# First attention: keys and queries as 64x64 products in four quarters of the array, two shared banks, another order of work

## The reference, cut to what matters

```python
q = einsum('oi,bil->bol', Wq, layernorm(x)) + bq      # k, v likewise from ctx
scores = einsum('hbdk,hbek->hbde', qh, kh) / 8        # 8 heads of 64 columns, 64 x 64 scores
x = x + Wo @ (softmax(scores) @ v) + bo
logits = layernorm(x) @ W_gate + b_gate               # top 2 of 8 experts, for the next phase
```

## Time and profile before

| | before |
|---|---|
| median of 3 runs | 995.98 us (995.69, 995.98, 999.72) |
| the profiled execution | 999.03 us, its span 997.2 us |
| PE busy over the span | 917.3 us (92%) |
| DVE, ACT, POOL busy | 440.8, 344.0, 290.4 us |
| scores of the first tile to the count product behind the last rank | 12.43 to 157.78 us |
| first work of PE for the experts | 169.97 us |
| clock granted to PE, mean | 0.949 |

### The profile page before, as it was taken

The page is one execution under the profiler, slowest core; times in us unless marked ns, Lnnn a source line. Parts: engine busy times, 40 slices in busy tenths (PEclk is TensorE's granted clock), DMA queues, the critical chain, the costliest instruction groups (busy, mean ns, idle before and its releaser), DMA issues. The chain is left out here.

```text
span 997.2 us, 17352 instructions
## 1 busy us (share of the span) xinstructions
PE 917.3 (92%) x6049; PEld 760.0 (76%) x6050; DVE 440.8 (44%) x888; ACT 344.0 (35%) x535; POOL 290.4 (29%) x416
## 2 busy tenths in 40 slices
PE   5999973999995889999999984999999999999997
PEld 4888863777774778888888863888788878878886
DVE  4888874333432546666666651212222222222112
ACT  3656631333331335565566542222111112111111
POOL 4678863000003554465564320211302000202000
PEclk9999985999997959999999985999999999999999
DMA  8566544444446532433433225111003000302001
GB/s 263 180 223 223 183 139 161 163 148 155 149 150 215 182 109 75 136 101 101 135 90 92 72 80 157 32 53 51 1 11 106 11 1 12 94 1 85 1 1 42
DMA packets 53431, 104.26 MB, mean 105 GB/s; under 512 B 7955, under 2 KB 8979, under 8 KB 53235
## 3 DMA queue, kind: packets, MB, share of 16 engines
q1 hardware_dynamic: 46594, 84.33, 26.6%
q0 software_dynamic: 5120, 16.78, 5.1%
q10 hardware_dynamic: 1648, 2.23, 0.6%
HBM read 65.83 MB, written 37.49 MB: 104 GB/s over the span
## 5 line engine op out<-in xcount | busy, mean ns | idle before, releaser
L1709 DVE SCALAR_TENSOR_TENSOR d_hid<-d_pup,d_b_up,d_silu 128x512 f32<-128x512 f32 (+1 forms) x44 | 33.0, 751 | 238.2 <-PE d_pup L1638 238.2
L1599 ACT ACTIVATE d_silu<-d_pgate,d_b_gate 128x512 f32<-128x512 f32 (+1 forms) x44 | 30.3, 689 | 154.7 <-PE d_pgate L1638 154.7
L985 POOL DMA_INDIRECT c_y_in<-expert_results,y_at x32 | 32.0, 999 | 152.9 <-POOLq L98 144.9
L1570 POOL TENSOR_TENSOR d_x_res<-d_x_res,d_b_down 128x512 f32<-128x512 f32 x16 | 21.2, 1350 | 188.2 <-DMA d_x_res<-x_after_attention 188.2
L1636 PE MATMUL d_pgate<-d_nT_hi,gate_up_hi 128*128 128x512 f32 (+1 forms) x176 | 71.5, 406 | 1.4 <-DVE d_nT_lo L1698 1.4
L1606 ACT ACTIVATE d_hid_hi<-d_hid 128x512 fp32r<-128x512 f32 (+1 forms) x44 | 27.8, 632 | 125.8 <-DVE d_hid L1709 125.8
L1638 PE MATMUL d_pgate<-d_nT_hi,gate_up_lo 128*128 128x512 f32 (+1 forms) x176 | 70.3, 400 | 0.0
L1637 PE MATMUL d_pgate<-d_nT_lo,gate_up_hi 128*128 128x512 f32 (+1 forms) x176 | 70.0, 398 | 0.0
L1636 PE MATMUL d_pup<-d_nT_hi,gate_up_hi 128*128 128x512 f32 (+1 forms) x176 | 69.7, 396 | 0.0
L1668 PE MATMUL d_pdown<-d_down_hi,d_hid_hi 128*128 128x512 f32 (+1 forms) x176 | 69.5, 395 | 0.0
L1638 PE MATMUL d_pup<-d_nT_hi,gate_up_lo 128*128 128x512 f32 (+1 forms) x176 | 69.3, 394 | 0.0
(11 more groups left out here) (227 smaller groups left out, 2077.8 us busy)
## 6 DMA issues: line engine op xcount, KB each, us to landing
b_rows<-expert_rows SPq DMA_DIRECT2D x39, 256.0 KB, 2.7
expert_results<-b_result SPq DMA_DIRECT2D x39, 256.0 KB, 2.0
a_wstage<-L_ffn_W_e SPq DMA_DIRECT2D x16, 512.0 KB
c_stage<-gate_up SPq DMA_DIRECT2D x16, 344.0 KB, 3.4
a_x<-x SPq DMA_DIRECT2D x16, 256.0 KB
a_ctx_in<-ctx SPq DMA_DIRECT2D x16, 256.0 KB
x_after_attention<-a_x SPq DMA_DIRECT2D x16, 256.0 KB
c_x<-x_after_attention SPq DMA_DIRECT2D x16, 256.0 KB, 2.9
```

What stands on the lines that cost most here:

```text
L985: pool.indirect_dma_start(out=y_in[:, 2 * (t % 2) + k, :], out_offset=None, in_=shared["ys"], in_offset=bass.IndirectOffsetOnAxis(ap=share ...
L1709: dve.scalar_tensor_tensor(hid[0:w, s % 2, :], pup[s % 2][0:w, :], b_up[0:w, i:i + 1], silu[0:w, s % 2, :], ALU.add, ALU.mult).then_inc(hi ...
```

## The change

- Keys and queries are no longer four products with a 128x128 weight each. Each is sixteen products of 64 rows, 64 columns and 64 moving columns: batch b (the rows of the array) and head parity r (its columns) pick one of the four quarters, in the order (0,0), (1,1), (0,1), (1,0).
- Both go to one tensor of two banks, `pkq`, batch b in bank b. So queries of a tile wait until its keys have been copied out, and keys wait for the copy of the queries before.
- The transposed normed result goes to `pt`, the bank of the transposed probabilities, in place of `pk`.
- Another order of the calls on PE, DVE and ACT. On PE: scores, keys, rank, values, transpose of the normed result, projection, queries, transpose of probabilities, logits, attention. In pvy the values of tile m+1 now come ahead of the projection of tile m-1, which waits until they have been copied out.

```diff
-        pk, pq, pvy, ps, pt, pr = (pb(n) for n in ("pk", "pq", "pvy", "ps", "pt", "pr"))
-        po = stack.enter_context(nc.psum_tensor("a_po", [P, 2, 512], F32))
+        pvy, ps, pt, pr = (pb(n) for n in ("pvy", "ps", "pt", "pr"))
+        pkq, po = stack.enter_context(nc.psum_tensor("a_pkq", [P, 2, 512], F32)), stack.enter_context(nc.psum_tensor("a_po", [P, 2, 512], F32))
...
# ACT, an iteration
-                if tile(m):
-                    high_part(m)
-                    exponent(m)
-                    keep_probT(m)
                 if tile(m + 1):
                     keep_v(m + 1)
+                if tile(m):
+                    exponent(m)
                 if tile(m - 2):
                     keep_xT(m - 2)
+                if tile(m):
+                    keep_probT(m)
+                    high_part(m)
...
# PE
+            def in_quarters(rows, w):
+                for j in range(4):
+                    for b, r in ((0, 0), (1, 1), (0, 1), (1, 0)):
+                        k, head = slice(64 * b, 64 * b + 64), 2 * j + r
+                        mm = pe.matmul(pkq[64 * r:64 * r + 64, b, 64 * j:64 * j + 64], rows[k, 64 * head:64 * head + 64],
+                                       w[k, k], start=True, stop=True)
+                return mm
...
# make_k
-                want(pe, k_kept, t)
-                want(pe, xt_kept, t - 3)
-                for j in range(4):
-                    mm = pe.matmul(pk[:, P * j:P * j + P], ctx_in[:, t % 3, P * j:P * j + P], wk[:, :], start=True, stop=True)
+                want(pe, q_kept, t)
+                mm = in_quarters(ctx_in[:, t % 3, :], wk)
# make_v
-                want(pe, x1_ready, t - 1)
+                want(pe, x1_ready, t - 2)
# make_q
-                want(pe, q_kept, t)
...
+                pe.wait_ge(k_kept, t + 1)
+                mm = in_quarters(xn[:, t % 2, :], wq)
# transpose_probs
+                want(pe, xt_kept, t - 1)
# project
-                if tile(t + 1):
-                    pe.wait_ge(v_kept, t + 2)
+                if tile(t + 2):
+                    pe.wait_ge(v_kept, t + 3)
# transpose_x
-                if tile(t + 3):
-                    pe.wait_ge(k_kept, t + 4)
+                if tile(t + 1):
+                    pe.wait_ge(pt_kept, t + 2)
...
# PE, an iteration, after
                     make_scores(m)
                     make_k(m + 1)
                     make_rank(group_ending(m - 3))
                     make_v(m + 1)
                     transpose_x(m - 2)
                     project(m - 1)
                     make_q(m + 1)
                     transpose_probs(m)
                     make_logits(m - 2)
                     make_attn(m)
# DVE, an iteration, after: sort, find, mark and add_marks of m-3 stay first, then
                     max_scores(m)
                     shift_scores(m)
                     keep_k(m + 1)
                     add_region(g), pick_ranks(g), sum_ranks(g), round_ranks(g)
                     add_residual(m - 1)
                     keep_q(m + 1)
                     sum_x1(m - 1), average_x1(m - 1)
                     sum_x(m + 3), average_x(m + 3)
                     invert_sums(m), keep_attn(m)
```

More of the change, by code:

```diff
@@ L365, in keep_xT @@
                 want(act, l_made, t)
-                act.activation(xT[:, :], pk[:, :], ACT.Copy).then_inc(xt_kept, 1)
+                act.activation(xT[:, :], pt[:, :], ACT.Copy).then_inc(xt_kept, 1)
             def high_part(t):
@@ L410, in make_q @@
                 pe.wait_ge(xn_ready, t + 1)
-                want(pe, q_kept, t)
-                for j in range(4):
-                    mm = pe.matmul(pq[:, P * j:P * j + P], xn[:, t % 2, P * j:P * j + P], wq[:, :], start=True, stop=True)
+                pe.wait_ge(k_kept, t + 1)
+                mm = in_quarters(xn[:, t % 2, :], wq)
                 mm.then_inc(q_made, 1)
@@ L461, in transpose_x @@
                 for j in range(4):
-                    mm = pe.transpose(pk[:, P * j:P * j + P], xn2[:, t % RING, P * j:P * j + P], ident[:, :])
+                    mm = pe.transpose(pt[:, P * j:P * j + P], xn2[:, t % RING, P * j:P * j + P], ident[:, :])
                 mm.then_inc(xt_made, 1)
@@ L491, in _ @@
                     make_scores(m)
-                if tile(m - 1):
-                    project(m - 1)
                 if tile(m + 1):
                     make_k(m + 1)
-                    make_q(m + 1)
-                if tile(m):
-                    transpose_probs(m)
+                if group_ending(m - 3) is not None:
+                    make_rank(group_ending(m - 3))
                 if tile(m + 1):
@@ L502, in _ @@
                     transpose_x(m - 2)
-                if group_ending(m - 3) is not None:
-                    make_rank(group_ending(m - 3))
+                if tile(m - 1):
+                    project(m - 1)
+                if tile(m + 1):
+                    make_q(m + 1)
+                if tile(m):
+                    transpose_probs(m)
+                if tile(m - 2):
+                    make_logits(m - 2)
                 if tile(m):
                     make_attn(m)
-                if tile(m - 2):
-                    make_logits(m - 2)
             pe.wait_ge(seen_ready, len(GROUPS))
@@ L526, in by_position, with made @@
             def by_position(ap):
-                return ap.rearrange("p (j o) -> p j o", o=64)
-            every_bk, every_bq = (b[:, :].rearrange("p (x o) -> p x o", x=1).to_broadcast([P, 8, 64]) for b in (bk, bq))
+                return ap.rearrange("p (j b o) -> p b j o", b=2, o=64)
+            def made():
+                return pkq[:, :, 0:256].rearrange("p b (j o) -> p b j o", o=64)
+            every_bk, every_bq = (b[:, :].rearrange("p (x y o) -> p x y o", x=1, y=1).to_broadcast([P, 2, 4, 64]) for b in (bk, bq))
             def keep_k(t):
@@ L535, in keep_k @@
                 want(dve, s_made, t)
-                dve.tensor_tensor(by_position(kT[:, :]), by_position(pk[:, :]), every_bk, ALU.add).then_inc(k_kept, 1)
+                dve.tensor_tensor(by_position(kT[:, :]), made(), every_bk, ALU.add).then_inc(k_kept, 1)
             def keep_q(t):
@@ L542, in keep_q @@
                 want(dve, s_made, t)
-                dve.tensor_tensor(by_position(qT[:, :]), by_position(pq[:, :]), every_bq, ALU.add).then_inc(q_kept, 1)
+                dve.tensor_tensor(by_position(qT[:, :]), made(), every_bq, ALU.add).then_inc(q_kept, 1)
             def max_scores(t):
@@ L640, in _ @@
                     shift_scores(m)
-                if tile(m - 1):
-                    add_residual(m - 1)
                 if tile(m + 1):
                     keep_k(m + 1)
[L645 to L649, removed]
                 if g is not None:
@@ L654, in _ @@
                     round_ranks(g)
+                if tile(m - 1):
+                    add_residual(m - 1)
+                if tile(m + 1):
+                    keep_q(m + 1)
+                if tile(m - 1):
+                    sum_x1(m - 1)
+                    average_x1(m - 1)
                 if tile(m + 3):
```

## The result

The kernel after takes 1010.96 us, the median of 4 runs (1005.99 to 1011.88); the kernel before, run on the same chip beside it, 997.69 (4 runs, 995.69 to 999.72). The ratio is 1.0123, with an interval from 1.008 to 1.0165: 1.2% slower, more than the spread of the runs. The forecast was 994.4 with a range to 1003. The profiled execution after took 1011.88 and has a span of 1010.1, so 12.9 more than before.

The account below looks back on a forecast made before the run. PE was taken to bound an iteration at 8.06, and afterwards the cycle PE, DVE, PE, ACT, PE at 8.37. Start +1.0, twelve iterations +1.8 and tail -4.4 gave -1.6: 994.4 from 995.98, range 987 to 1003.

Parts of the forecast that it names:

- the term of the twelve iterations: First attention, scores of tile 3 to those of tile 15: 12 x 8.37 = 100.4 against 98.63, +1.8.
- rival B: First attention: `low_part` on POOL holds DVE's `pick_ranks` in every tile; +13 in twelve iterations, 1007.5; chance 0.1.
- Two stalls: PE in each iteration: 0.38 ahead of the rank product for `add_marks`, 0.6 ahead of the projection for `keep_v`.
- The clean iteration: First attention, one tile's scores to the next: 8.37, where PE's own work is 7.23.
- Rival A: Keys and queries: column halves of the same rows don't run side by side, 0.030 a pass; +6.6, 1001.0; chance 0.2.
- Rival C: First attention: one of the two stalls is absent, POOL's 7.8 bounds; 12 x 0.57 less, 987.6; chance 0.22.
- Start: Start to the scores of tile 3: second iteration 7.3 against 6.34, +0.4 ahead of it, -0.4 in the third; +1.0.
- Tail: Behind tile 15's scores: no collision and attention at full clock, -2.7; clock staying up behind it, 1.7; together -4.4.
- Or if anything behind 170 us moves: Sign against the prediction: it is wrong if anything after 170 us moves.
- the sum: Whole kernel: +1.0 + 1.8 - 4.4 = -1.6, giving 994.4 on the median of 995.98; forecast's chance 0.42.

Follow-up runs that it names:

- with zeros: Kernel after, with POOL writing zeros into the experts' low part (two memsets) in place of the subtraction; one run, 1008.24, twelve iterations 102.77.
- with the wait: Kernel after, with POOL's `low_part` of tile m-1 waiting until `round_ranks` of tile m-3 is done; 1005.12, ratio 1.0041 to the kernel before.
- the ranks later on DVE: Kernel after, with `pick_ranks`, `sum_ranks` and `round_ranks` moved behind `average_x1` on DVE; 1008.65, ratio 1.0082 to the kernel before.
- the kernel before with the wait: Kernel before, with POOL's `low_part` of tile m-1 waiting until `add_marks` of tile m-3 is done; 995.27, ratio 0.9949 to the kernel before.
- the kernel with 128x128 products: Kernel after's order and waits, but keys and queries as four 128x128 products each; 1017.27, ratio 1.0169 to the kernel before.
- the clean tile above: A tile no hold lengthens, from kernel after with `pick_ranks`, `sum_ranks`, `round_ranks` behind `average_x1` on DVE; that kernel 1008.65, ratio 1.0082.
- the other order: Kernel after's quarters, PE, ACT and DVE reordered, ACT's `norm_x` earlier, `high_part` later, `low_part` waiting for ranks; fastest kernel measured, 996.58, ratio 0.9921 to before.

## Why the prediction was wrong

**The step that failed** is the term of the twelve iterations, "12 x 8.37 = 100.4 against 98.63: +1.8", which counts no held DVE instruction in any of them. It measured +17.5. The collision was looked for in the tail alone, and there for the marks alone: "POOL comes to that `low_part` about 3.9 after the scores and the marks are done at 2.0, so I expect no collision". For the tail this held: POOL came 4.95 after the scores of tile 15, and nothing was held there. For the steady tiles the collision was left to rival B, with a chance of 0.1 and a price of 13. B was the truth: 13.4 of the 17.5 in the twelve iterations go when `low_part` is made harmless in either of two ways (102.77 with zeros, 102.76 with the wait). That its price fits so well is in part luck: 3.2 of the 13.4 lie in the first iteration, where the marks are held and the clock falls, which B did not have. The places that B worked out were right to 0.2: `pick_ranks` at 3.94, forecast 4.1 to 4.35, and `low_part` at 4.38, forecast 4.4. With these a hold would still seem to be missed by 0.1 to 0.3, and I leaned on that. Two facts were not in the account.

First, DVE is held from a point ahead of the start that the profile shows for POOL's instruction. The cast of two neighbouring tiles, the first held, the second not:

```profile
72.58 3.08 DVE L640 CAST a_ati<-a_at_kept 128x2 int32<-128x2 f32 x1
73.25 2.39 POOL L303 TENSOR_TENSOR expert_w_lo<-a_wstage,expert_w_hi 128x1024 fp32r<-128x1024 f32 x1
...
82.27 0.96 POOL L310 DMA_INDIRECT expert_rows<-a_xn,a_ati  x1 [0.30 <-issue]
82.56 0.17 DVE L640 CAST a_ati<-a_at_kept 128x2 int32<-128x2 f32 x1
83.25 2.39 POOL L303 TENSOR_TENSOR expert_w_lo<-a_wstage,expert_w_hi 128x1024 fp32r<-128x1024 f32 x1
```

0.67 ahead it is held, 0.69 ahead it is not; the other tiles agree (held at 0.66 to 0.68, free at 0.69 to 0.84), each with a scatter right ahead of `low_part`. Is it then the scatter that holds DVE? Two runs answer: the ranks later on DVE, and the kernel before with the wait. In both, `mark_experts` begins 0.39 into a scatter that starts at 152.50 and at 132.83; in the second, `low_part` still waits for the marks:

```profile
152.89 2.98 DVE L607 TENSOR_TENSOR a_hot_kept<-a_chosen,a_expert_no 128x16 f32<-128x16 uint32 x1
153.48 2.35 POOL L303 TENSOR_TENSOR expert_w_lo<-a_wstage,expert_w_hi 128x1024 fp32r<-128x1024 f32 x1
```

```profile
133.22 0.17 DVE L596 TENSOR_TENSOR a_hot_kept<-a_chosen,a_expert_no 128x16 f32<-128x16 uint32 x1
133.82 2.35 POOL L304 TENSOR_TENSOR expert_w_lo<-a_wstage,expert_w_hi 128x1024 fp32r<-128x1024 f32 x1
```

Held in the one, free in the other, at the same place in the scatter. So it is `low_part`, and the early hold comes only where `low_part` waits for nothing but the scatter ahead of it. The row for this was there before: `mark_experts` began at 134.81 and `low_part` at 135.47, 0.66 later, and I read only its end. A window of 2.4 was really one of 3.07 in this order of POOL's work, and `pick_ranks`, 0.44 ahead, is well within it.

Second, the cast in `round_ranks` is held too, though it has one input. With it, `mark_experts` (L607), `pick_ranks` and, in the kernel with 128x128 products, the sum into `seenb` (3.06 at 53.90) four instructions were held, and a DVE that has been pushed back once lands with the next one in the next `low_part`. That "a stalled DVE pushes POOL back too" was my reason against B. By the rows it is true (in all seven long iterations with both, the cast starts 0.66 to 0.71 ahead of `low_part`, held or not), and I take it as the reason why the state lasts: both move together. No run tests that by itself.

The Trainium skill's page "SBUF — State Buffer", Who interferes with whom, names both kinds: two-input instructions against a GpSimd instruction that reads SBUF, and copies and casts, which can run in a mode that takes the port pair shared with GpSimd and then contend with it. The zeros agree with it, `pick_ranks` at 0.18 (145.85) and the cast at 0.90 beside a memset; that the cast ran in that mode no row shows. I had cited the first half of that section and not asked which DVE instructions fall under the second.

**The other steps**, from the clean tile above (92.58 to 101.14):
- Two stalls: rank at 1.97 after a stall of 0.41 (forecast 2.02 and 0.38), projection at 4.03 after 0.43 (4.04 and 0.6; PE is free at 3.60 and not at 3.45, so the stall is shorter and its end the same). Right: chains of latency that the old order never showed could be added up from its rows.
- The clean iteration is 8.56, forecast 8.37. The missing 0.2 is in the four groups behind the projection: queries 0.63 (0.60 was forecast), transposes 0.58 (0.53), logits 1.30 (1.22), attention 0.99 (0.95). Three of the four border on a change of shape. The change without the holds costs 4.1 in twelve (102.76 against 98.63), forecast 1.8.
- Rival A, 0.030 a pass, is refuted: the queries cost 0.63 with the change of shape behind them (forecast 0.48 and 0.12), where A has 0.96 without it. Rival C didn't come.
- Start +0.9, forecast +1.0.
- Tail -1.5, forecast -4.4. Tile 15's attention starts 6.83 after its scores (7.28 before; within 7.5 was forecast), and PE keeps its full clock until 164, also as forecast. But behind that attention PE waits for the marks 1.81 and 1.47 and for the norm 1.77 us, so a faster PE only waits longer: 15.21 behind the attention, 16.28 before. With the wait on `low_part` the old order's tail is 18.93 and the new one's 22.15. A likely reason is that the rank product now stands near the head of PE's list and all else queues behind its wait; no run tests it, and the other order, where it stands behind the transposes, has 22.65.
- "Or if anything behind 170 us moves": layer 1's attention did, by 4.0, and that is the spread of that stretch and not the change's.

So the sum was +1.0 + 1.8 - 4.4, and is +0.9 + 17.5 - 1.5 + 0.1, less 4.1 from elsewhere, 12.9.

What stays open: why the hold begins 0.68 ahead of the recorded start, while the scatter still runs (POOL's spans are rough, so its instruction may simply begin earlier than shown); the tail of the fastest kernel, which no run took apart; and what makes layer 1's attention vary by 9 us.

## What to carry to other kernels

Before an order of work is changed, list the instructions of DVE that another engine can hold and the long instructions of POOL, and lay both on one time axis; a margin of some tenths between them is no margin, and one cheap wait on POOL (here 13 us of the twelve iterations and some 8 of the whole in one order, 5 to 6 of the whole in the other) is worth more than luck in the order. A phase that was PE's bound stops being so as soon as work is taken off PE and waits for other engines are put ahead of the rest; cheaper products then pay for idle time. Where a trace shows one long specimen of a short instruction, read both of its ends against the neighbour's, not only the end.

## What the hardware showed that I had not expected

- A DVE instruction on 2 columns was held for 3.08 us beside POOL's 128x1024 subtraction of 2.39, since the hold began up to 0.68 ahead of that one's recorded start. The scatter ahead of it (0.96) was not what held it: the 2-column cast at 82.56 ran in 0.17 in the midst of one, and `mark_experts` at 133.22 too. But a few casts beside a scatter took longer than 0.17 and ended just ahead of its end, 0.44 at most (the ranks later on DVE, at 163.18).
- A 64x64 pass (one of the two that a float32 product takes) with 64 columns costs at most 0.02 us in four quarters (32 in 0.63 with the way out of the shape) and 0.030 in two diagonal ones. The groups of 128x128 on both sides of it cost 0.10 and 0.06 more than beside their like; of the 0.27 that a group of 0.90 gained, 0.13 were left in an iteration.
